# Splitting the shared FFN of a cross-attention and mixture-of-experts kernel: 17 tiles beside the slot search, 15 among the experts

## What is computed

```python
scores = jax.nn.softmax(xf @ gate_w.T, axis=-1)
topk_w, topk_idx = jax.lax.top_k(scores, K)
...
gx = xp[buf_tok]                                  # (64, 128, 512)
gu = jnp.einsum('ech,ehi->eci', gx, gate_up_proj) # gate and up, 192 wide each
g, u = jnp.split(gu, 2, axis=-1)
eo = jnp.einsum('eci,eih->ech', jax.nn.silu(g) * u, down_proj) * buf_w[..., None]
routed = jnp.zeros((T + 1, h), x.dtype).at[buf_tok.reshape(-1)].add(eo.reshape(-1, h))[:T]
shared = jax.nn.silu(xf @ shared_gate_w.T) * (xf @ shared_up_w.T) @ shared_down_w.T
x = x + routed + shared
```

## Time and profile before

| | |
|---|---|
| median of three runs | 1348.53 us (1340.64 to 1351.66) |
| the profiled execution | 1346.4 us |
| its span, first to last instruction | 1344.4 us |
| busy in the span | PE 1169.3 us (87%), DVE 806.9 (60%), POOL 681.8 (51%), ACT 517.9 (39%) |
| mean granted TensorE clock | 0.948 of 2.4 GHz |
| moved by DMA | 194.73 MB, mean 145 GB/s |

### The profile page before, as it was taken

How to read it: one execution, slowest core, us unless ns; L and a number is a source line. 1 busy time by engine, 2 the same in 40 slices (tenths; PEclk the granted TensorE clock), 3 DMA queues, 4 the chain that set the end, 5 groups by cost and what they waited for, 6 DMA issues and landing times. The chain is left out here.

```text
span 1344.4 us, 18158 instructions
## 1 busy us (share of the span) xinstructions
PE 1169.3 (87%) x5305; PEld 885.2 (66%) x5305; DVE 806.9 (60%) x1240; ACT 517.9 (39%) x980; POOL 681.8 (51%) x388
## 2 busy tenths in 40 slices
PE   3999999999999999997599999998878787878780
PEld 2777777777777777776588899965545455545450
DVE  1687777787778787786489945444333333343340
ACT  5454545555555555534121222133323333233230
POOL 5988888988888988870000000212334333343332
PEclk9999999999999999999799999999898988898885
DMA  6222333322333322313473443569999999999973
GB/s 186 83 76 77 92 98 98 92 75 77 98 98 98 94 74 78 96 49 108 95 205 108 117 112 105 146 174 271 246 251 245 254 255 258 238 258 251 238 175 44
DMA packets 118266, 194.73 MB, mean 145 GB/s; under 512 B 17888, under 2 KB 55456, under 8 KB 118112
## 3 DMA queue, kind: packets, MB, share of 16 engines
q1 hardware_dynamic: 103904, 158.76, 41.4%
q0 software_dynamic: 14336, 35.66, 12.8%
HBM read 150.55 MB, written 43.79 MB: 145 GB/s over the span
## 5 line engine op out<-in xcount | busy, mean ns | idle before, releaser
L936 POOL TENSOR_TENSOR ring<-vT,cT 128x1024 f32<-128x1024 f32 x128 | 249.0, 1956 | 78.5 <-ACT vT L710 46.5
L390 PE MATMUL Y<-split,toep 128*128 128x512 f32 x576 | 250.4, 435 | 9.6 <-POOL split L944 9.6
L944 POOL TENSOR_TENSOR split<-ring,split 128x1024 fp32r<-128x1024 f32 x96 | 229.4, 2390 | 0.0
L392 PE MATMUL Y<-split,toep 128*128 128x512 f32 x576 | 228.4, 396 | 0.0
L391 PE MATMUL Y<-split,toep 128*128 128x512 f32 x576 | 228.2, 396 | 0.0
L1055 DVE TENSOR_TENSOR z<-Y,cT 128x1024 f32<-128x1024 f32 x128 | 156.1, 1220 | 114.6 <-PE Y L394 79.1
L980 POOL DMA_INDIRECT stage<-xn_rows,idx_i x64 | 67.8, 1059 | 298.0 <-issue 283.2
L608 PE MATMUL Y<-ring,xT 128*128 128x384 f32 x512 | 204.7, 526 | 5.0 <-DMA ring<-in_L_ffn_down_proj_dram 5.0
L1060 DVE TENSOR_REDUCE o<-z 128x128 f32<-128x1024 f32 x128 | 154.4, 1206 | 1.1
L521 PE MATMUL Y<-split 128*128 128x384 f32 x768 | 152.9, 348 | 1.6 <-DVE split L1114 1.6
L521 PEld LDWEIGHTS Y<-split 128*128 128x128 f32 x768 | 134.2, 193 | 1.9 <-DVE split L1229 1.9
(11 more groups left out here) (135 smaller groups left out, 1695.7 us busy)
## 6 DMA issues: line engine op xcount, KB each, us to landing
ring<-_L_ffn_gate_up_proj_dram SPq DMA_DIRECT2D x64, 768.0 KB
ring<-in_L_ffn_down_proj_dram SPq DMA_DIRECT2D x64, 384.0 KB
gr<-filters SPq DMA_DIRECT2D x32, 512.0 KB, 3.7
stage<-in_x_dram SPq DMA_DIRECT2D x32, 256.0 KB, 3.5
stage<-in_ctx_dram SPq DMA_DIRECT2D x32, 256.0 KB, 3.7
x_rows<-stage SPq DMA_DIRECT2D x32, 256.0 KB, 2.9
xn_rows<-xn SPq DMA_DIRECT2D x32, 256.0 KB, 3.2
xn<-xn_rows SPq DMA_DIRECT2D x32, 256.0 KB, 3.7
```

The source lines that it names most:

```text
L390: pe.matmul(y, high, kv[:, s, 0, a, n], start=(a == 0), stop=False)
L392: last = pe.matmul(y, low, kv[:, s, 0, a, n], start=False, stop=(a == c))
L936: pool.tensor_tensor(to.rearrange("p (b j i) -> p b j i", i=NH, j=NH), a, d, ALU.mult).then_inc(kvp_ready, 1)
L944: pool.tensor_tensor(kv[:, s, 1, c, :], kvp[c], kv[:, s, 0, c, :].bitcast(F32), ALU.subtract).then_inc(kv_ready, 1)
```

## The change

Stage B runs for tiles 0 to 16 only (`TB2` = 17). The slot search is packed into these: three pairs per two tiles for t = 2 to 12, the move at tile 13 (`MOVE_AT` = 12), then six, six and four of the small pairs in tiles 14 to 16, and the list right behind. Tiles 17 to 31 are cut into stages and put among the experts, four experts to a tile (`SPAN` = 4): `shared_gate`, `shared_up`, `b_turn_hid`, `shared_down` and `b_turn` of the next tile stand each behind the work of one expert, in banks Y[2] and Y[3].

The output is made otherwise. Stage A stores x1 straight to `out`; `x1_rows` is gone. Tiles 0 to 16 load x1 from there and store y over it. The shared result of tiles 17 to 31 is evacuated by ACT (`shared_out`) and added to `out` by POOL like an expert's (`add_shared`, indices `idx_t` from a new constant). Every add is now two: `out` is seen as rows of 256 numbers, and columns 0 to 255 and 256 to 511 have each their own indices and their own semaphore, `added[0]` and `added[1]`. Within a column half each add waits for the one before; the two halves don't wait for each other.

The 16 DMAs of `sc_all` move from SP's list to POOL's, ahead of the gathers. The loops of stages B and C are written out. Buffers of stage C (`c_d`, `c_hTs`, `c_sg`, `c_hidden`, `eo`) move, since those of stage B now live beside them.

```diff
-MOVE_AT = NF + 2
-LIST_AT = NT - 3
+TB2 = 17
+SPAN = 4
+MOVE_AT = 12
...
-        eo = [y[:, 0, :], y[:, 1, :], w[:, 0, :], w[:, 1, :]]
+        eo = [w[:, 0, :], w[:, 1, :], z[:, 0, :], z[:, 1, :]]
...
+        def stage_of(e):
+
+            n = e + 2
+            return n % SPAN, TB2 + n // SPAN
+
+        def adds_before(e):
+
+            return e + sum(1 for t in range(TB2, NT) if SPAN * (t + 1 - TB2) < e)
...
-                sp.dma_start(rows(x1_rows, h), x1[:, s, :]).then_inc(x1_out[s], 16)
+                sp.dma_start(rows(out[0:T, :], h), x1[:, s, :]).then_inc(x1_out[s], 16)
...
+            for e in range(E):
+                q, t = stage_of(e)
+                if q == 2 and t + 3 < NT:
+                    b_load_xn(t + 3, (t + 3) % 2)
+                if e + NW < E:
+                    sp.wait_ge(c_down, e + 1)
+                    weights(sp, e + NW, e % NW)
...
+            def c_iteration(e):
+                q, t = stage_of(e)
                 pe.wait_ge(c_xT_sb, e + 1)
...
+                c_up(e, 1)
+                if q == 2 and t + 1 < NT:
+                    pe.wait_ge(c_xT_sb, e + 2)
+                    b_turn(t + 1, (t + 1) % 2)
+                if e:
+                    c_out(e - 1)
+                if q == 0 and t < NT:
+                    shared_gate(t)
+                elif q == 1 and t < NT:
+                    shared_up(t)
+                elif q == 2 and TB2 < t <= NT:
+                    shared_down(t - 1)
+                elif q == 3 and t < NT:
+                    b_turn_hid(t, t % 2)
+
+            shared_gate(TB2)
+            shared_up(TB2)
+            c_turn(0)
...
+            halves = out.rearrange("t (a l) -> (t a) l", a=2)
+
+            def add(e, a):
                 pool.wait_ge(eo_ready, e + 1)
                 if e:
-                    pool.wait_ge(added, e * 16)
+                    pool.wait_ge(added[a], adds_before(e) * 16)
...
+            def add_shared(t, a):
+                pool.wait_ge(shared_ready, t + 1 - TB2)
+                pool.wait_ge(added[a], (adds_before(SPAN * (t + 1 - TB2)) + 1) * 16)
...
             for e in range(E):
                 if e + NG - 1 < E:
                     fetch(e + NG - 1)
-                add(e)
-            pool.wait_ge(added, E * 16)
+                for a in range(2):
+                    add(e, a)
+                t = TB2 + e // SPAN - 1
+                if e % SPAN == 0 and TB2 <= t < NT:
+                    for a in range(2):
+                        add_shared(t, a)
```

More of the change, by code:

```diff
@@ L322, in _ @@
             sp.dma_start(place, c_order).then_inc(order_in, 16)
[L323 to L350, removed]
+            for t in range(TB2):
+                if t == 2:
+                    sp.wait_ge(sh_lo, n_turn)
+                b_iteration(t, t % 2, fetch_x1=(t < TB2), expert=(t - 2 if 2 <= t < 2 + NW else None))
+                if t == MOVE_AT + 1:
+                    sp.wait_ge(first_ready, NF)
+                    sp.dma_start(both[:, CAP:], firsts[E:2 * E, :]).then_inc(half_in, 16)
+            b_store(TB2 - 1, (TB2 - 1) % 2)
+            b_load_xn(TB2 + 2, TB2 % 2)
+            for e in range(E):
[5 more added lines that the diff above has]
+                    weights(sp, e + NW, e % NW)
         @block.tensor
@@ L660, in _ @@
+            shared_gate(TB2)
+            shared_up(TB2)
+            c_turn(0)
+            for e in range(E):
+                c_iteration(e)
+            c_turn_hid(E - 1)
+            c_out(E - 1)
         @block.scalar
@@ L902, in c_iteration @@
-            def c_iteration(e, r, last=False):
-                s = r % 2
-                if not last:
-                    c_evacuate(e + 1, 1 - s, first=(among(e, 0)))
-                if not among(e, 0):
-                    c_evacuate_hid(e - 1, 1 - s)
-                c_gate(e, s)
-                c_down_high(e, r)
-            c_evacuate(0, 0, first=True)
-            for e in range(NW):
-                c_iteration(e, e)
-            with act.Fori(1, E // NW - 1) as i:
-                for r in range(NW):
-                    c_iteration(i * NW + r, r)
@@ L917, in _, with c_down_high @@
[L917 to L919 removed]
+                act.activation(c_hTs[:, e % 2, 0, :, :].rearrange("p c n -> p (c n)"), TB[0:IH, 0:2 * P], ACT.Copy).then_inc(c_hT_sb, 1)
+            def c_down_high(e):
+                r = e % NW
+                act.wait_ge(weights_in[r], (e // NW) * 32 + 32)
+                if e > 1:
+                    act.wait_ge(c_down, e - 1)
+                act.activation(c_d[e % 2][:, 0, :, :].rearrange("p c n -> p (c n)"), ring[0:IH, r, NC * SI:], ACT.Copy).then_inc(c_d_high, 1)
@@ new lines, in shared_out, with c_iteration @@
+            def shared_out(t):
+                s = t % 2
+                act.wait_ge(b_down, t + 1)
+                if t - 2 < TB2:
+                    act.wait_ge(y_out[s], landed(t - 2, s, 16))
+                else:
+                    for a in range(2):
+                        act.wait_ge(added[a], (adds_before(SPAN * (t - 1 - TB2) + 1)) * 16)
+                act.activation(y[:, s, :], Y[2][:, :], ACT.Copy).then_inc(shared_ready, 1)
+            def c_iteration(e):
+                q, t = stage_of(e)
+                if q == 0 and TB2 < t <= NT:
+                    b_evacuate_hid(t - 1, (t - 1) % 2)
+                if q == 1 and t < NT:
+                    b_gate(t, 0, Y[2])
+                if q == 3 and TB2 < t <= NT:
+                    shared_out(t - 1)
+                if e + 1 < E:
+                    c_evacuate(e + 1)
+                if e:
+                    c_evacuate_hid(e - 1)
+                c_gate(e)
+                if q == 2 and t + 1 < NT:
+                    b_evacuate(t + 1, (t + 1) % 2)
+                c_down_high(e)
@@ L922, in _ @@
+            b_gate(TB2, 0, Y[2])
+            c_evacuate(0)
+            for e in range(E):
+                c_iteration(e)
+            c_evacuate_hid(E - 1)
         @block.gpsimd
@@ L1369 @@
+            for e in range(E):
+                c_iteration(e)
+            c_hidden_low(E - 1)
+            c_result(E - 1)
 _INS = ['x', 'fside_S2_0', 'ctx_2048', 'L0_xattn_k', 'L0_ffn_gate_w', 'L0_ffn_gate_up_proj', 'L0_ffn_down_proj',
```

372 lines of the change are left out of this document (195 added, 177 removed).

## The result

| | before | after |
|---|---|---|
| median, four runs each side by side | 1347.6 us | 1376.7 us (1371.94 to 1378.34) |
| ratio | | 1.021, interval 1.017 to 1.025 |
| span of the profiled execution | 1344.4 us | 1369.8 us |
| first turn of stage C | 882.96 us | 818.09 us |
| PE busy | 1169.3 us | 1171.5 us |

The change makes the kernel slower by 2.1%. It was forecast to be faster, 1286 us in a range of 1250 to 1338. What came is the second rival, which had said 1372.

A forecast was written before the change was run, and what follows sets the result against it. Stage B was taken as PE-bound, stage C as near-bound by its add chain and the DMA engines. Stage B 78 us shorter (stage C from 805) plus stage C 479 (18 longer) gave span 1284, so 1286 us, range 1250 to 1338.

The forecast's parts named there:

- Rival 2: Stage C: 15 more chained adds at 7.0 us cost 105 us against 78 saved; span 1372, turning point 6.65; chance 0.09.
- A chain paces stage C: Stage C before: add issue (1.6 us), transfer and landing (5.4), then the next add, 7.0 us a step.
- The DMA engines stand at 95% of it: Stage C before: 254 GB/s in the middle against a ceiling taken as 268 GB/s, so DMA is close to binding.
- Stage B, 78 us earlier: Stage B after: terms sum to 155 us, first turn of stage C at 805 instead of 883.
- the term of two-pair tiles: Stage B, tiles 2 to 12: five tiles with two search pairs, DVE 11.8 us each, above PE's 7.4.
- rival 4: Stage B: two-pair tiles cost 14 us, so 11 us later, 1295; counted within the forecast's 0.60.
- the hole at tile 3: Stage B: PE's 12.2 us wait for a load of xn, forecast to be gone with the probability writes on POOL.
- Stage C, 479 us: Stage C after: 434 us of DMA at 257 GB/s plus 10 of start and 35 of tail, 18 us longer.
- P: Stage C: time between neighbouring adds of one column half, put at 5.3 us for the chain alone, 5.9 with DMA.
- The DMA engines decide, by 45 us over the chain alone: Stage C after: 479 us by the DMA engines against 434 us by the chain of half adds alone.
- The prediction's own sign of error: Stage C: half adds landing 6.6 us or more apart with DMA share well under 0.95 would show it wrong.
- Rival 1: Stage C: a half add's landing hardly shrinks, halving saves 0.3 us, P = 6.7; span 1349, no change; chance 0.08.

The follow-up runs named there:

- e10: Kernel before, with odd experts added to a second tensor in a chain of their own, never joined to the output: span 1283.7 us.
- e6: Kernel before, with only the 16 writes of the probabilities moved from SP's list to POOL's: 1336.1 us, ratio 0.9922.
- e8: Kernel before, adds split into column halves and only the left half added, the right left out: span 1290.8 us.
- e1: Kernel before, with nothing changed but each add cut into two column halves with a chain each: 1346.6 us, ratio 0.9988.
- e2: Changed kernel with the halves joined again, full 2048-byte rows and one chain of 79 adds: 1382.6 us, ratio to before 1.0232.
- e12: e1's kernel with POOL's list reordered to left half, gather, right half: 1348.9 us, ratio 1.0014.
- e5: Changed kernel with the 15 shared tiles computed but their adds left out: 1290.1 us, span 1288.3.
- e4: Kernel before, with the weights of experts 4 to 63 not loaded: 1263.3 us, span 1261.4.
- e9: Kernel before, with down weights loaded for the first four experts only, 0.39 of 1.18 MB per expert not moved: 1288.6 us.
- e7: e2 with the 15 shared results kept in DRAM and added behind the last expert's add without waits between them: 1344.2 us, ratio to before 0.9979.
- e11: e7 with 26 tiles in stage B, one search pair per tile, and only six late shared tiles: 1322.2 us, ratio to before 0.9828.
- e3: Changed kernel, with the weights of experts 4 to 63 not loaded: 1251.7 us, span 1249.6.

## Why the prediction was wrong

**What bounded the kernel before: right in the first half.** "A chain paces stage C" is shown by e10: opened, it gives 0.9 us per expert. "The DMA engines stand at 95% of it" was wrong: 268 GB/s was the rate of one 10 us window, not a ceiling, as e10 carries 277 over 270 us. That is 9% over the 254 GB/s of the middle of the stage.

**Stage B, 78 us earlier: 65 came.** The shape was right (DVE sets the pace in packed tiles) and the term of two-pair tiles was mis-sized, 13.4 us instead of 11.8 and near the 14 us of rival 4. The forecast summed DVE's work and left out that PE, made to wait 4.6 us, comes back at a lower clock: its down part takes 3.89 us instead of 2.24, and DVE's sum with x1 waits 1.35 us for it (681.33). That is 1.35 of the 1.6 us missing; the rows fit, though no run isolated it. Together with the rest of the hole at tile 3 (4.9 us stay, "is gone" was wrong; e6 leaves the same 4.8), tiles 2 to 12 took 113.4 us (649.57 to 763.01) instead of 103. From the turn at 777.28 to the end of the stage it was 40.8 us instead of 37, with two more down parts at 4.2 us.

**Stage C, 479 us: 551.7 came.** The failed step is the one on P: "half of that away gives 5.3". It took the half's saving from a count of engine time in the empty tail (2.0 us, of which half goes) and scaled it up for company (3.4). The tail itself agrees: 5.5 less 1.0 is 4.5, and 4.5 came. In company a lone half gains 0.85 us (e8), and when its partner follows nothing is left: 7.2 in e1, 6.95 after, 6.84 with whole rows (e2). A further term set at nothing was the order of POOL's list: the sum let each half run as a chain of its own, and the trace has right halves holding left ones (0.56 us per expert in e1). "The DMA engines decide, by 45 us over the chain alone" fell with this step: the chain alone is 21 + 78 x 6.75 = 548 us, 4 more come at its ends, and the engines, held back by the chain, ran at 214 GB/s. The prediction's own sign of error (half adds 6.6 us or more apart with a DMA share well under 0.95) is what the windows show: 6.95 and 0.87.

**Rival 2 was right in mechanism and nearly in size.** It said 105 us of new chain against 78 saved and 1372; the trace has 90 against 65 and 1369.8. The part it gave to the place in POOL's list is not needed for the slowdown, as e2 has whole rows and the same step; for the halves it is partly borne out (0.32 us per step after, 0.56 in e1), and e12, which moves only the gather, does not test it. Its turning point moves with stage B: (1344.4 - 818.1 - 25) / 78 = 6.4 us. e5 gives the price per shared add, 5.4 us; the trade would be even at 65/15 = 4.3, or at 3.7 with the 9 us of PE's work taken off the 65. It had 0.09, because the argument against it ("a half moves half the bytes") was taken for a fact about latency.

**Rival 1.** Its P of 6.7 came within 0.05 of the mean, for a reason that does not hold: it let each half gain 0.3 us, and a half gains 1.0 in the tail, 0.85 alone in company (e8) and nothing measurable with its partner in company; the mean of 6.75 has the short steps of the tail in it. The Trainium skill ("DMA: Bandwidth & Descriptors", "Anatomy of one DMA — SWDGE (gpsimd) path") has a DMA take about 2.0 us and bytes/436e3 on top; as an estimate from that, half an add saves 0.3 us. No measured value agrees with it: two lie above and one below.

**What held.** PE had the room: e5, with all of PE's shared work and none of its adds, has a stage C of 470 us, 9 more than before. That its span of 1288.3 is near the 1284 forecast is luck: stage B ended 13 us later than forecast, and stage C, without the adds, was 9 us shorter than the 479. PE's total busy time is unchanged. ACT's `shared_out`, eight experts behind the add it waits for, cost nothing: among its waits of after is none for an add worth a row.

**What stays open.** Where each expert has one step, the step grows with the bytes moved per step (rate times step in the middle of the stage): 5.68 us at 0.56 MB (e4), 6.03 at 1.36 (e9), 6.15 at 1.61 (e8), 7.0 at 1.78 (before), 7.6 at 1.86 (e7); e11 lies under the row with 6.9 at 1.80. These runs differ in other things too, but the reading would explain e7, whose shared results go out to DRAM beside the adds. The changed kernel does not fit it: 6.95 us at 1.49 MB, and e2 6.84 at 1.48, with engines less full than before. Why is not settled. e3 was bound by PE and could not show a half alone without company. Joining two outputs, as e10 would need, was not tried.

## What to carry to other kernels

Price a step that waits for its own landing in the traffic where it will run, not in an empty tail, and don't count on two halves from one list and queue to land sooner than the whole: here they didn't in company, and the list made them wait for each other. Before work is moved to a stage with idle engines, count what it adds to that stage's serial chain: here 15 tiles of PE work were nearly free and their 15 chained adds cost 81 us, while updates that touch different rows can leave the chain and go unwaited behind it at 1.86 us each. Moving 15 of them out did not pay (e7, the adds left in the chain slowed down), moving six did (e11). Side work packed until it overtakes the engine it hides behind costs more than the overlap says, as PE here came back from pauses of 3.6 to 4.9 us at a lower clock, and long runs of DMA issues belong in a queue nobody waits on (11 us here).

## What was unexpected of the hardware

- After a pause of 4.6 us PE was granted 0.56 of full clock over the next 3.9 us, and nine matmuls of 128x512 took 3.89 us instead of 2.24.
- The DMA share is no measure of what is left: 0.98 stood at 254 GB/s before, and 1.07 at 277 GB/s in e10, over 270 us.
- POOL's issue of an accumulating DMA takes 1.55 us for 128 rows of 1024 bytes and for 128 rows of 2048, so two halves cost twice the issue of a whole.
- The 1.18 MB of weights moved per expert make a step of whole adds 1.3 us longer (5.68 us in e4, 7.0 before), though add and weights are issued by different engines.
